# Adaptive-norm attention and mixture of experts: slots turned between the halves of the up products, and two ranks of results added on VectorE

## The reference, cut to what matters

```python
# per token: 4 of 32 experts, weights topk_w; per expert at most CAP slots are kept
h = silu(einsum('ech,ehf->ecf', buf, w1)) * einsum('ech,ehf->ecf', buf, w3)
ob = einsum('ecf,efh->ech', h, w2)
y = where(keep, ob[flat_e, slot], 0)
out = (y.reshape(n, K, H) * topk_w[:, :, None]).sum(1)
shared = silu(x @ shared_gate) * (x @ shared_up) @ shared_down
x = x + gb * (out + shared)
```

## Time and profile before

| | us |
|---|---|
| three timed runs | 176.85, 175.35, 176.83; median 176.83 |
| the profiled execution | 175.42 |
| its span, first to last instruction | 173.7 |
| busy: PE, PEld | 147.5, 102.1 |
| busy: DVE, ACT, POOL | 108.9, 62.4, 55.4 |

### The profile page before, as it was taken

The page is one execution under the profiler, slowest core; times in us unless marked ns, Lnnn a source line. Parts: engine busy times, 40 slices in busy tenths (PEclk is TensorE's granted clock), DMA queues, the critical chain, the costliest instruction groups (busy, mean ns, idle before and its releaser), DMA issues.

```text
span 173.7 us, 2811 instructions
## 1 busy us (share of the span) xinstructions
PE 147.5 (85%) x938; PEld 102.1 (59%) x938; DVE 108.9 (63%) x386; ACT 62.4 (36%) x167; POOL 55.4 (32%) x77
## 2 busy tenths in 40 slices
PE   0198769999999899997598969996999989879993
PEld 0153534887547767685274624886666656568882
DVE  2679964836955688799884598382566664321563
ACT  3257578633055526375243623012333333200000
POOL 7319700499500000000000000777077776440000
PEclk9999999999999999999999999999999999999999
DMA  4999999999999942001000110244113331118995
GB/s 130 340 321 405 423 400 357 348 349 347 349 348 348 348 136 70 0 0 38 30 4 0 44 60 4 68 123 115 36 37 101 94 73 69 50 46 298 411 319 181
DMA packets 21808, 31.34 MB, mean 180 GB/s; under 512 B 2032, under 2 KB 17942, under 8 KB 21794
## 3 DMA queue, kind: packets, MB, share of 16 engines
q1 hardware_dynamic: 20354, 27.71, 46.8%
q0 software_dynamic: 1440, 3.45, 7.2%
HBM read 23.65 MB, written 8.26 MB: 184 GB/s over the span
## 4 chain that ended last, share of the span: by engine, by line
PE 50%; DVE 32%; ACT 7%; issue 5%; DMA 3%; SPq 1%; DVEq 0%; ACTq 0%
PE bank L1054 16%; PE bank L1351 10%; PE bank L1397 6%; PE bank L1391 4%; DMA w_sb<-in_L_wmod_dram 3%; PE bank L1370 3%; DVE bmax L797 3%; DVE st L708 2%; DVE rows L818 2%; PE bank L1184 2%; PE bank L1361 2%; DVE base L811 2%; PE bank L1328 2%; PE bank L1158 2%; PE bank L1162 2%
## 5 line engine op out<-in xcount | busy, mean ns | idle before, releaser
L444 POOL DMA_INDIRECT arena<-token_rows,gather_idx x16 | 16.4, 1025 | 67.2 <-DVE gather_idx L907 62.6
L1351 PE MATMUL bank<-w_sb,arena 128*64 128x128 f32 x256 | 17.3, 278 | 3.4 <-ACT arena L655 1.3
L1351 PEld LDWEIGHTS bank<-w_sb,arena 128*64 128x64 f32 x256 | 13.9, 136 | 7.7 <-issue 4.1
L453 POOL DMA_INDIRECT results<-aT,res_idx x14 | 14.0, 999 | 11.0 <-DVE aT L997 7.9
L1184 PE MATMUL bank<-arena 128*128 128x256 f32 x72 | 17.2, 382 | 0.3 <-issue 0.3
L1184 PEld LDWEIGHTS bank<-arena 128*128 128x128 f32 x72 | 13.1, 190 | 2.5 <-issue 0.9
L1054 PE MATMUL bank<-w_sb,h2T 128*128 128x512 f32 x12 | 7.6, 769 | 8.2 <-DMA w_sb<-in_L_wmod_dram 8.2
L1017 DVE TENSOR_TENSOR h2T<-h2T,bank 128x256 f32<-128x256 f32 x8 | 3.4, 421 | 15.7 <-ACT h2T L672 15.7
L537 ACT ACTIVATE prob<-bank,nmax 128x512 f32<-128x512 f32 (+3 forms) x12 | 6.9, 581 | 12.4 <-DVE nmax L801 12.4
L1397 PE MATMUL bank<-w_sb,ident 128*128 128x256 f32 x48 | 10.6, 382 | 0.0
L556 ACT ACTIVATE h2T<-bank,modc 128x128 f32<-128x128 f32 x16 | 6.4, 455 | 11.5 <-PE bank L1192 11.5
(11 more groups left out here) (154 smaller groups left out, 302.2 us busy)
## 6 DMA issues: line engine op xcount, KB each, us to landing
w_sb<-in_L_ffn_w_dram SPq DMA_DIRECT2D x12, 1024.0 KB, 12.3
results<-prob SPq DMA_DIRECT2D x1, 4096.0 KB, 16.7
w_sb<-results SPq DMA_DIRECT2D x7, 512.0 KB, 6.4
token_rows<-rows SPq DMA_DIRECT2D x8, 144.0 KB
xin<-in_L_attn_x_dram SPq DMA_DIRECT2D x4, 256.0 KB, 4.3
w_sb<-in_L_wmod_dram SPq DMA_DIRECT2D x1, 1024.0 KB, 9.5
out_dram<-base SPq DMA_DIRECT2D x8, 128.0 KB, 3.7
w_sb<-in_L_attn_qkv_dram SPq DMA_DIRECT2D x1, 768.0 KB, 7.1
```

The source lines that it names most:

```text
L444: nc.gpsimd.indirect_dma_start(out=slot_in[:, r, :], out_offset=None, in_=rows_d, in_offset=bass.IndirectOffsetOnAxis(ap=gather_idx[:, r:r ...
L453: nc.gpsimd.indirect_dma_start(out=results_d, out_offset=bass.IndirectOffsetOnAxis(ap=res_idx[:, r:r + 1], axis=0), in_=ob[:, g % 4, (r % ...
L1351: last = t.matmul(bank[4 + g % 2][CAP * side:CAP * side + CAP, o:o + F], slotT[:, k, CAP * e:CAP * e + CAP], w[:, e, k, :], start=(k == 0) ...
```

## The change

On TensorE, `turn_slots(g + 1)` moves between the two halves of the up products of group g, behind `turn_hid(g - 1)`. ScalarE evacuates slots ahead of silu, and VectorE ahead of the hidden product; the copies of scores come behind that product. In the last group the down products of group 6 stand between the two halves, and the two halves of the fourth `shared_down` stand around the turn of the last hidden values. The seventh part of the shared up products moves ahead of `positions(2)` and the eighth ahead of `map_slots(1, ...)`. The results of groups 0 to 2 (modulo 4) get memory of their own in the arena; `SHD_BANK` and the waits follow. Gathers run 5 groups ahead of give-backs in place of 4. The score sums and the last two shared additions move on VectorE. In the last stage TensorE adds ranks 0 and 1 (in the last tile 0 to 2) and VectorE the others; the way back takes tile 0 last. The diff, without the functions on VectorE that only change places (`expert_hid` is the hidden product as a function):

```diff
-        ob = aT[:, :, :].rearrange("p f n -> p (f n)").rearrange("p (b s) -> p b s", b=4)
+        ob = [take(512) for _ in range(3)] + [aT[:, 0, 0:512]]
...
-        SHD_BANK = [bank[b] for b in (1, 2, 4, 5)]
+        SHD_BANK = [bank[b] for b in (1, 2, 3, 0)]
+        PE_RANKS = [2] * (NT - 1) + [3]
...
-                        in_=ob[:, g % 4, (r % 2) * H:(r % 2 + 1) * H], in_offset=None,
+                        in_=ob[g % 4][:, (r % 2) * H:(r % 2 + 1) * H], in_offset=None,
...
-            AHEAD = 4
+            AHEAD = 5
...
                 if g >= 1:
                     hid_evac(g - 1)
+                if g + 1 < EGROUPS:
+                    slot_evac(g + 1)
                 act.wait_ge(up_mm, g + 1)
                 if g >= 2:
                     act.wait_ge(hid_done, g - 1)
                 a.activation(act_h[:, g % 2], bank[4 + g % 2][:, :].rearrange("p (r w f) -> p r w f", r=2, w=2)[:, :, 0, :],
                              ACT.Silu).then_inc(silu_done, 1)
-                if g + 1 < EGROUPS:
-                    slot_evac(g + 1)
...
             shared_hid(1, 1)
             shared_add(0)
             shared_add(1)
-            score_sums()
-            shared_add(2)
 
             def slot_evac(g):
                 dve.wait_ge(slotT_mm, g + 1)
+                v.tensor_scalar(slotT[:, 1, 256 * g:256 * g + 256], bank[1][:, 0:256],
+                                modc[:, 0, 1:2], modc[:, 1, 1:2], ALU.mult, ALU.add).then_inc(slotT_dve, 1)
+
+            def scores_of_slots(g):
+
                 for side in range(2):
                     half = slice(CAP * side, CAP * side + CAP)
                     step(v.tensor_copy(slot_score[half, 2 * g:2 * g + 2],
                                        slot_flat[half, (2 * g) * (ROW + 2) + H + side::ROW + 2][:, 0:2]))
-                v.tensor_scalar(slotT[:, 1, 256 * g:256 * g + 256], bank[1][:, 0:256],
-                                modc[:, 0, 1:2], modc[:, 1, 1:2], ALU.mult, ALU.add).then_inc(slotT_dve, 1)
...
-            slot_evac(0)
-            shared_add(3)
-            dve.wait_ge(base_done, NB)
-            dve.wait_ge(scale_done, 1)
-            for g in range(EGROUPS):
...
-                if g + 1 < EGROUPS:
-                    slot_evac(g + 1)
-                if g >= 1:
...
+            slot_evac(0)
+            shared_add(2)
+            for g in range(EGROUPS - 1):
+                slot_evac(g + 1)
+                expert_hid(g)
+                scores_of_slots(g)
+                if g == 0:
+                    score_sums()
+                else:
                     expert_evac(g - 1)
                 if 1 <= g < 5:
                     back_map(2 * g - 2)
                     back_map(2 * g - 1)
+            scores_of_slots(EGROUPS - 1)
+            expert_evac(EGROUPS - 2)
+            expert_hid(EGROUPS - 1)
             expert_evac(EGROUPS - 1)
-
+            shared_add(3)
+            dve.wait_ge(base_done, NB)
+            dve.wait_ge(scale_done, 1)
 
             for i in range(NT):
                 dve.wait_ge(y_loaded[i], 16)
                 if i == NT - 1:
                     dve.wait_ge(y_rest_loaded, 16)
-                chain(v.scalar_tensor_tensor(out=base[:, i, :], in0=yin[i][:, H * 3:H * 4],
-                                             scalar=scale2[:, i:i + 1], in1=base[:, i, :], op0=ALU.mult, op1=ALU.add))
+                for k in range(PE_RANKS[i], TOPK):
+                    chain(v.scalar_tensor_tensor(out=base[:, i, :], in0=yin[i][:, H * k:H * k + H],
+                                                 scalar=scale2[:, i:i + 1], in1=base[:, i, :], op0=ALU.mult, op1=ALU.add))
...
-            def shared_down(j):
+            def shared_down(j, parts=(0, 1)):
 
                 pe.wait_ge(sh_hid, (2, 2, 4, 4)[j])
                 if j < 2:
                     pe.wait_ge(sh_silu, 2)
-                for i in range(2):
+                for i in parts:
                     tok = slice(P * (2 * j + i), P * (2 * j + i) + P)
                     last = product(SHD_BANK[j][:, H * i:H * i + H], [(aT[:, f, tok], shd_sb[:, f, :])
                                                                      for f in range(FS // P)])
-                last.then_inc(shd_mm, 1)
+                if 1 in parts:
+                    last.then_inc(shd_mm, 1)
...
             shared_up_part(SH_ORDER[5])
+            shared_up_part(SH_ORDER[6])
             positions(2)
-            shared_up_part(SH_ORDER[6])
-            map_slots(1, BATCHES[2][0], NT, 3)
             pe.wait_ge(sh_silu, 1)
             shared_up_part(SH_ORDER[7])
+            map_slots(1, BATCHES[2][0], NT, 3)
             pe.wait_ge(shd_scaled, 1)
...
-                    pe.wait_ge(base_done, 2)
+                    pe.wait_ge(base_done, 1)
...
-            def expert_up(g):
-
-
-                if g % 2 == 0:
-                    pe.wait_ge(experts_loaded[g // 2], 48)
-                pe.wait_ge(slotT_act, g + 1)
-                pe.wait_ge(slotT_dve, g + 1)
-                if g >= 2:
-                    pe.wait_ge(hid_done, g - 1)
-                else:
-                    pe.wait_ge(base_done, 3 + g)
-                for r in range(2):
-                    for what, w in enumerate((w1_sb, w3_sb)):
-                        if g >= 1 and (r, what) == (1, 1):
-                            turn_hid(g - 1)
-                        o = 256 * r + P * what
-                        for k in range(KT):
-                            for side in range(2):
-                                e = 4 * g + 2 * r + side
-                                last = t.matmul(bank[4 + g % 2][CAP * side:CAP * side + CAP, o:o + F],
-                                                slotT[:, k, CAP * e:CAP * e + CAP], w[:, e, k, :],
-                                                start=(k == 0), stop=(k == KT - 1))
-                last.then_inc(up_mm, 1)
+            def expert_up(g, r):
+
+                if r == 0:
+                    if g % 2 == 0:
+                        pe.wait_ge(experts_loaded[g // 2], 48)
+                    pe.wait_ge(slotT_act, g + 1)
+                    pe.wait_ge(slotT_dve, g + 1)
+                    if g >= 2:
+                        pe.wait_ge(hid_done, g - 1)
+                for what, w in enumerate((w1_sb, w3_sb)):
+                    o = 256 * r + P * what
+                    for k in range(KT):
+                        for side in range(2):
+                            e = 4 * g + 2 * r + side
+                            last = t.matmul(bank[4 + g % 2][CAP * side:CAP * side + CAP, o:o + F],
+                                            slotT[:, k, CAP * e:CAP * e + CAP], w[:, e, k, :],
+                                            start=(k == 0), stop=(k == KT - 1))
+                if r == 1:
+                    last.then_inc(up_mm, 1)
 
             def turn_hid(g):
                 pe.wait_ge(hid_done, g + 1)
                 if g >= 2:
                     pe.wait_ge(hidT_done, g - 1)
+                else:
+                    pe.wait_ge(base_done, 2 + g)
...
             turn_slots(0)
-            shared_down(3)
-            for g in range(EGROUPS):
-                expert_up(g)
-                if g + 1 < EGROUPS:
-                    turn_slots(g + 1)
+            for g in range(EGROUPS - 1):
+                expert_up(g, 0)
+                if g >= 1:
+                    turn_hid(g - 1)
+                turn_slots(g + 1)
+                expert_up(g, 1)
                 if g >= 1:
                     expert_down(g - 1)
-            turn_hid(EGROUPS - 1)
-            expert_down(EGROUPS - 1)
+            last_g = EGROUPS - 1
+            turn_hid(last_g - 1)
+            expert_up(last_g, 0)
+            expert_down(last_g - 1)
+            expert_up(last_g, 1)
+            shared_down(3, (0,))
+            turn_hid(last_g)
+            shared_down(3, (1,))
+            expert_down(last_g)
 
             pe.wait_ge(ob_done, EGROUPS)
             pe.wait_ge(back_done, NT)
             pe.wait_ge(hidT_done, EGROUPS)
-            for i in range(NT):
+            for i in list(range(1, NT)) + [0]:
+                if i == 0:
+                    pe.wait_ge(base_done, NB)
                 for r in range(2):
-                    t.matmul(bank[i][:, 0:H], back[:, r, i, :], ob[:, BACK % 4, H * r:H * r + H], start=(r == 0), stop=False)
+                    t.matmul(bank[i][:, 0:H], back[:, r, i, :], ob[BACK % 4][:, H * r:H * r + H], start=(r == 0), stop=False)
             for i in range(NT):
                 pe.wait_ge(y_loaded[i], 16)
-                for k in range(3):
+                for k in range(PE_RANKS[i]):
                     if i == NT - 1 and k == 2:
                         pe.wait_ge(y_rest_loaded, 16)
-                    last = t.matmul(bank[i][:, 0:H], ident[:, :], yin[i][:, H * k:H * k + H], start=False, stop=(k == 2))
+                    last = t.matmul(bank[i][:, 0:H], ident[:, :], yin[i][:, H * k:H * k + H], start=False,
```

(12 more changed lines are left out.)

6 lines of the change are left out of this document (removed).

## The result

The changed kernel takes 170.12 us (median of 4 runs, 168.82 to 170.81) against 176.6 before (4 runs, 175.35 to 176.85): a ratio of 0.9638, 95% interval 0.9555 to 0.9721. That is 6.5 us less; I had forecast 2.9 less and a time of 173.8, with 172.0 as the low end. The direction was right and the size wrong by more than a factor of two. Times of the experiments are medians of all their runs, and the ratios leave out single runs more than 1.5% above the fastest of their kernel, without which e2 took 169.38, e7 170.47, e8 168.79, e9 169.63, e11 168.34, e14 175.4, e15 174.01 and e16 169.42 us.

The account below looks back on a forecast made before the run. TensorE, with idle waits, was taken to bound the expert stage, and VectorE the changed kernel's end. Gains 2.2 + 1.95 - 1.35 (tail) + 0.5 - 0.4 = 2.9 us gave 173.8 us, range 172.0 to 175.5.

Parts of the forecast that it names:

- Start of the stage: Expert stage start: gathers 0.3 later, TensorE waits 1.2 before the first slot turn, group 1 starts 2.2 us earlier.
- Six periods: Expert groups 1 to 6: idle pieces gone, period 4.11 us for 4.44, saving 1.95 us.
- term of 1.95: Saving over the six loop periods in the forecast sum: 24.7 us for 26.62.
- POOL: POOL's transfer queue: one more group of gathers ahead of give-backs; give-backs alone take 2.6 of 4.11, catching up by group 4.
- rival (c): POOL give-backs fall behind, loads of ranks start at 155.9 as before; time 175.7; chance 0.04.
- Tail, transfers, end: After the loop: way back from 150.5, loads from 150.8 holding nothing, VectorE bounding the end at 1.44 us a tile.
- (a): VectorE's end at 1.20 us a tile, waits between additions costing nothing; time 172.3; chance 0.08.
- (b): Loop waits stay, another wait on VectorE's queue replacing them; period 4.44, gain 0.95, time 175.9; chance 0.13.
- (d): Slower: new idle 1.2 us at 112.7 drops TensorE to its low clock; two groups so would give 182; chance 0.04.

Follow-up runs that it names:

- e2: Changed kernel with two more, long-satisfied semaphore waits in front of each quarter of the up products; 169.94 us.
- e7: Changed kernel with the seventh and eighth shared up parts back in their old places; 170.97 us.
- e8: Changed kernel with all gathers ahead of the first give-back on POOL; 169.73 us.
- e9: Changed kernel with two and three ranks in turn on TensorE, VectorE adding two and one; 169.88 us.
- e11: Changed kernel with VectorE's last stage reordered: next tile's first rank ahead of each final addition, the second behind it; 168.71 us.
- e14: Kernel before, with hidden values turned right in front of the slot turn and ScalarE's silu ahead of its hidden copy; 175.64 us.
- e15: Changed kernel with the slot turn split in two around the fourth quarter of up products, six tile-shape changes a group for two; 174.07 us.
- e16: e11 again, in five rounds, for its interval; 169.7 us (6 runs), ratio 0.9587 to the kernel before.
- e1: Changed kernel with the hidden turn moved into the middle of the second half of up products, four tile-shape changes a group for two; 171.51 us.
- e5: Changed kernel with three ranks of every tile on TensorE and one on VectorE; 170.27 us.
- e4: Changed kernel with slots evacuated behind silu on ScalarE and behind hidden product and score copies on VectorE, the old order; 178.96 us.
- e13: Changed kernel with the edits of e9, e11, e8 and e6 together; 171.79 us.
- e6: Changed kernel with the whole fourth shared down product right behind the third, none in the last group's waits; 170.54 us.

## Why the prediction was wrong

- **Start of the stage.** Right in kind, a little too dear: the seventh part fills the idle time and ends almost with the mask, so gathers come 0.07 later and not 0.3 (second issue at 111.41 - 1.38 = 110.03 for 109.96), the TensorE gap before the first slot turn is 0.88 for 1.2, group 0 at 115.08 shifted for 115.3. The gain of 2.2 by group 1 became 2.6, since the halves of up products, too, are shorter than 1.06 (0.92 and 0.98 above).
- **Six periods: the step that failed.** "I count the idle pieces as gone and the period as 4.11. The bounds are 4.11 and 4.44." The waits went, as said, and up products never waited for VectorE's slots again. But I took 4.11 as TensorE's least work in a group, adding up pieces of the old chain as if a piece had the same length in any order. Four of the five stood behind a change of the weights' width. With two changes in place of four, and no stop for the slots in which the down products run out, the period is 3.57: 0.54 a group, 2.7 us over the five periods between the first and sixth turn of hidden values. The term of 1.95 in the sum measures 26.62 - 22.19 = 4.43, the wait of 0.40 included. e1, e2 and e15 show the part of the shape changes, 0.3 to 0.4 of the 0.54; the part of 0.15 from the end of the down products is read from the traces and was not tested alone. The lower bound should have been lower: in an unbroken run the 32 up records take 0.92 + 0.98 us start to start, where I had 1.53 + 0.59.
- **POOL.** I had it catch up by group 4; it never pauses. It costs 0.40 here, and of rival (c) I was right only in that the end does not hang on it. e14 shows what it costs with four groups ahead: 1.6.
- **Tail, transfers, end.** Right to 0.1 us in sum: the tail's order, the way back, loads that hold nothing, a period of 1.44 set by VectorE, and two ranks on VectorE worth nothing (e5). From the turn of hidden 5 to the way back it is 10.9 us for a forecast of 10.8; that is in part luck, since the wait of 0.40 lies in it and shorter pieces make up for it.
- **Rivals.** (a) 1.20 a tile did not come with this order (a wait for the direct predecessor costs 0.13), but is what e11 gets by another order. (b) did not happen; e4 shows that it would have, at 2.6 us slower than before, had the two queues stayed. (d), the low clock behind the new idle at 112.7, did not decide, but it is no fiction: it was seen at that place in the profiles of e2, e8 and e15. In e15 the turn of slots there took 1.04 us for 0.59 at a clock of 0.50, and e2, whose loop has the same period, needs 34.83 us from the first slot turn to the way back for 33.75. The row from which I took the price does not show the low level: the profile's granted clock is 1.00 from 8 to 12 us.

## What to carry to other kernels

Price a stretch of TensorE by its records in an unbroken run, and count the changes between narrow (64) and full (128) weights separately, 0.15 to 0.2 us each here: putting transposes side by side was worth 0.3 to 0.4 us a group, as much as removing the wait (4.44 - 4.11). When the loop gets faster, go through the queues that had slack, POOL's issues above all (1.31 us each). And place an operation between two dependent VectorE operations: it saves 0.12 us a time at no cost.

## What the hardware showed that I had not expected

TensorE's granted clock falls in some executions and not in others of the same kernel, behind short idle pieces. In the changed kernel's profile, the idle of 2.03 us before the turn at 86.17:

```profile
86.17 0.44 PE L1204 MATMUL bank<-ident,rows 128*128 128x128 f32 x2 [2.03 <-DVE rows L819]
```

The same turn in the kernel before:

```profile
86.27 0.44 PE L1192 MATMUL bank<-ident,rows 128*128 128x128 f32 x2 [2.02 <-DVE rows L818]
```

The changed kernel's table by stages, 1 us each:

```profile
87.00:88.00 1.00, 1.00 (x5) 0.78 (x4) 0.93 (x3) 0.82 (x4) 0.00 (x0) 0.53 0.00 0
88.00:89.00 1.00, 1.00 (x4) 0.79 (x3) 0.21 (x1) 0.91 (x6) 0.00 (x0) 0.50 0.00 0
...
91.00:92.00 1.00, 1.00 (x6) 0.89 (x5) 0.56 (x3) 0.00 (x0) 0.00 (x0) 1.00 0.00 0
```

0.50 is the 1.2 GHz level, and the clock stands there from 87 to about 90.5. From this turn to the next shared products TensorE took 5.63 us where it took 4.15 before, 1.48 more; 0.10 it had been ahead, and 1.38 us are left. Before, with the same idle of 2.02 at the same place, the clock stayed at 1.00. The timed runs of the two kernels spread over 1.5 and 2.0 us, with mean clocks between 0.99 and 1.00, which fits this.

In e15, e2 and e8 it fell behind the start of the expert stage as well, where TensorE waits for the gather and then 0.7 to 0.85 for the slots. The wait for the gather was 1.01 to 1.07 us in these three profiles and 0.85 to 0.91 in those of the same order that kept their clock there. e15:

```profile
114.00:115.00 1.00, 0.07 (x1) 0.00 (x0) 0.00 (x0) 0.00 (x0) 0.89 (x1) 1.00 0.63 161
...
118.00:119.00 1.00, 1.00 (x6) 0.72 (x4) 0.00 (x0) 0.00 (x0) 0.79 (x1) 0.50 0.62 143
```

And in e13, whose tail is left with idle pieces of 0.94, 0.46 and 0.98 because nothing fills its waits, it fell at 148 for 6 us, into the way back (order of time on TensorE):

```profile
145.78 0.44 PE L1397 MATMUL bank<-ident,h2T 128*128 128x128 f32 x2 [0.94 <-DVE h2T L997]
146.68 1.08 PE L1406 MATMUL bank<-w_sb,prob 128*64 128x256 f32 x8 [0.46 <-ACT prob L663]
148.74 10.14 PE L1435 MATMUL bank<-aT,xin 128*128 128x256 f32 x32 [0.98 <-DVE aT L1008]
```

10.14 us for 7.17 is e13's loss; all its four runs had mean clocks of 0.97 to 0.98. e6 has the same idle pieces and kept its clock there in the profile, though its timed runs show 0.975 to 0.99. So the halves of the shared product in the last waits, worth nothing by their own time (e6), may be worth more for what they keep from happening. No run here shows that they do: the changed kernel's timed runs had mean clocks of 0.99 and more, e6's lower ones, but where the clock fell in e6's timed runs is not known.
